# A vision-transformer block on one core: the order of the grey, edge, normalisation and projection work, and the banks of its products

## What is computed

```python
gray = einsum('bchw,c->bhw', x, (0.2989, 0.587, 0.114))
h = abs(conv(gray, scharr)).sum(over the two filters) / 2      # 3 x 3 taps, padded by one
n = (h - mean) / sqrt(var + 1e-5)                              # by row of 256
q, k, v = n @ Wq + bq, n @ Wk + bk, n @ Wv + bv                # 16 heads of 16
q, k = q @ Wp, k @ Wp                                          # in each head
h = h + softmax(q @ k.T / 4) @ v
h = h + ffn(layernorm(h))                                      # fc1, silu, fc2, dequantised weights
```

## Time and profile before

| | us |
|---|---|
| median of 3 runs | 315.38 (314.59 to 318.14) |
| profiled execution | 317.39 |
| its span in the profile | 315.6 |
| PE busy in the span | 284.4 (90%) |
| DVE busy | 206.3 (65%) |
| ACT busy | 173.8 (55%) |
| POOL busy | 136.9 (43%) |

### The profile page before, as it was taken

How to read it: one execution, slowest core, us unless ns; L and a number is a source line. 1 busy time by engine, 2 the same in 40 slices (tenths; PEclk the granted TensorE clock), 3 DMA queues, 4 the chain that set the end, 5 groups by cost and what they waited for, 6 DMA issues and landing times.

```text
span 315.6 us, 6328 instructions
## 1 busy us (share of the span) xinstructions
PE 284.4 (90%) x2332; PEld 221.0 (70%) x2332; DVE 206.3 (65%) x415; ACT 173.8 (55%) x330; POOL 136.9 (43%) x268
## 2 busy tenths in 40 slices
PE   5599059889699998899999999999999999999996
PEld 5477047767577765666666666566899899899976
DVE  8586454855699988488889888662872742641432
ACT  2416476857063378377878768768444344344450
POOL 7250534531100014766286864217859489600000
PEclk9989759999999999599999999999999999999999
DMA  6828613178979794367568000000000200200201
GB/s 213 264 61 286 185 37 137 66 223 179 322 194 316 237 335 148 92 178 225 189 160 206 11 3 2 2 0 3 0 2 0 68 2 0 70 0 0 69 0 66
DMA packets 27310, 35.90 MB, mean 114 GB/s; under 512 B 5184, under 2 KB 16272, under 8 KB 27280
## 3 DMA queue, kind: packets, MB, share of 16 engines
q1 hardware_dynamic: 27184, 35.43, 37.3%
q10 hardware_dynamic: 96, 0.07, 0.1%
HBM read 24.42 MB, written 10.49 MB: 111 GB/s over the span
## 4 chain that ended last, share of the span: by engine, by line
PE 57%; DVE 9%; DMA 8%; ACT 7%; SPq 7%; POOL 5%; issue 4%; ACTq 1%; DVEq 0%; POOLq 0%
PE bank L1198 30%; PE bank L1327 7%; PE bank L1279 6%; PE bank L1302 4%; PE bank L1307 3%; PE bank L1345 3%; DMA bv<-in_L_attn_bv 3%; DVE negmax L909 3%; DMA wscale<-in_L_ffn_fc_scales 2%; SPq L427 2%; DMA halo_x<-in_x 2%; SPq L417 2%; PE bank L1216 1%; ACT xn L1083 1%; PE bank L1337 1%
## 5 line engine op out<-in xcount | busy, mean ns | idle before, releaser
L909 DVE TENSOR_REDUCE negmax<-bank 128x2 f32<-128x512 f32 x128 | 82.1, 684 | 6.9 <-PE bank L1279 6.6
L1109 ACT ACTIVATE probs<-bank 128x512 f32<-128x512 f32 x128 | 66.3, 603 | 29.1 <-PE bank L1307 29.1
L963 DVE TENSOR_TENSOR y_l<-yf,y_h 128x512 fp32r<-128x512 f32 x32 | 24.1, 754 | 38.6 <-ACT yf L1135 38.4
L1132 ACT ACTIVATE y_h<-bank,b1col 128x512 fp32r<-128x512 f32 x32 | 22.0, 687 | 47.7 <-PE bank L1198 47.6
L1198 PE MATMUL bank<-w_h,y_h 128*128 128x256 f32 x128 | 36.9, 289 | 1.1 <-DVE y_l L963 0.7
L1198 PE MATMUL bank<-w_l,y_h 128*128 128x256 f32 x128 | 36.2, 283 | 0.0
L1198 PE MATMUL bank<-w_h,y_l 128*128 128x256 f32 x128 | 36.2, 283 | 0.0
L1327 PE MATMUL bank<-probs,vals 128*32 128x256 f32 x512 | 35.1, 393 | 0.0
L1279 PE MATMUL bank<-ks,qs 48*128 48x256 f32 x256 | 32.6, 333 | 1.3 <-DVE negmax L909 0.7
L1279 PEld LDWEIGHTS bank<-ks,qs 48*128 48x128 f32 x256 | 19.8, 189 | 15.1 <-DVE negmax L909 6.1
L1307 PEld LDWEIGHTS bank<-qs,ks 48*128 48x128 f32 x256 | 24.9, 189 | 2.7
(11 more groups left out here) (158 smaller groups left out, 609.7 us busy)
## 6 DMA issues: line engine op xcount, KB each, us to landing
xr<-in_x SPq DMA_DIRECT2D x8, 768.0 KB, 8.5
qs<-qk_parts SPq DMA_DIRECT2D x48, 128.0 KB, 3.2
ks<-qk_parts SPq DMA_DIRECT2D x48, 128.0 KB, 3.3
qk_parts<-qk_h SPq DMA_DIRECT2D x16, 256.0 KB, 3.1
qk_parts<-qk_l SPq DMA_DIRECT2D x16, 256.0 KB, 3.2
wraw<-in_L_ffn_fc_q SPq DMA_DIRECT2D x4, 512.0 KB, 5.0
wscale<-in_L_ffn_fc_scales SPq DMA_DIRECT2D x4, 512.0 KB, 6.8
out<-osb SPq DMA_DIRECT2D x16, 128.0 KB, 1.8
```

Of the source, the lines that this page charges most:

```text
L909: eng.tensor_reduce(negmax[:, b % 2, u, v], entry_bank(key)[:, :].rearrange("p (t k) -> p t k", t=NT), AX.X, ALU.max, negate=True).then_in ...
L963: eng.tensor_tensor(y_l[:, p % 2, f], yf[:, n % 2], y_h[:, p % 2, f].bitcast(fp32), ALU.subtract).then_inc(s_y, 1)
L1109: eng.activation(probs[:, n % PBUF], p2[n % 4][:, :], ACT.Exp).then_inc(s_exp, 1)
L1132: eng.activation(y_h[:, p % 2, f], src, ACT.Silu, bias=b1col[:, f:f + 1])
```

## The change

In words, by engine:

- Banks: before `qkv(0, 0)` nothing changes for the eight tiles `tok(0)` and `tok(1)` (banks 4 to 7), but the cycle over all eight banks now begins at `xt(0, 0)` instead of at `qkv(0, 0)` and runs 0 to 7 in order, not 0, 1, 2, 3, 6, 7, 4, 5. From `qkv(1, 5)` on, banks 4 to 7 are taken in the order in which they were last used. PE waits for `s_wready` before `xt(0)` and not behind it. The second `keep_busy` has 12 transposes, not 8.
- SP: images 4 and 5 are requested ahead of the halo rows of group 1; the wait for POOL's zeroed halo goes in front of `stack_halo(1)`.
- POOL: V's weights are split behind `tok_rstd(0, .)`; `tok_rstd(2, t)` goes behind the grey of image 6 + t.
- DVE: halo_add(0) behind grey 1, halo_add(1) and halo_low(1) behind the weights and `xt_low(0)`; `pick` at the end of the front part; `gray_add(6)` behind `qkv_out(0, 1)`; the second tile's statistics of pair p + 2 behind `qkv_out(p, 4)`.
- ACT: image 1's scale ahead of the halo's; the edges of tile 0 of pair 1 in two halves, one between the two normalisations; gray_scale(6) ahead of `edge(2, 0)`; `xt_high` ahead of the edge of the second tile.

```diff
@@ -266,13 +266,18 @@
                     turns.extend(("xt", p + 1, kf) for kf in range(KE))
         turn = {key: n for n, key in enumerate(turns)}
 
-        fold_over, heads_begin = turn["qkv", 0, 0], turn["qkv", 1, 5]
+        fold_over, heads_begin = turn["xt", 0, 0], turn["qkv", 1, 5]
         turn_at, nth, uses = {}, {}, [[] for r in range(8)]
         for n, key in enumerate(turns):
-            if fold_over <= n < heads_begin:
-                r = (0, 1, 2, 3, 6, 7, 4, 5)[(n - fold_over) % 8]
+            if n < fold_over:
+                r = 4 + n % 4
+            elif n < heads_begin:
+                r = (0, 1, 2, 3, 4, 5, 6, 7)[(n - fold_over) % 8]
             else:
-                r = 4 + (n if n < fold_over else n - heads_begin) % 4
+
+                if n == heads_begin:
+                    upper = sorted(range(4, 8), key=lambda q: turn[uses[q][-1]])
+                r = upper[(n - heads_begin) % 4]
             turn_at[key], nth[key] = r, len(uses[r])
             uses[r].append(key)
         last_turns = [uses[4 + q][-1] for q in range(4)]
@@ -451,11 +456,10 @@
                 eng.dma_start(qk_bcol[:, i, :], src.rearrange("(m p) -> p m", p=P), allow_slow_non_contiguous=True).then_inc(s_wpd, 16)
             eng.wait_ge(s_border, 6)
             stack_halo(eng, 0)
-            eng.wait_ge(s_halo_z, 2)
+            load_x(4)
+            load_x(5)
             load_halo(eng, 1)
-            load_x(4)
             eng.dma_start(wv_src[:], Wv.rearrange("(k p) n -> p k n", p=P)).then_inc(s_wld, 16)
-            load_x(5)
             for t in range(NT):
                 eng.dma_start(bv2[:, t, :], bv.rearrange("(a n) -> a n", a=1).broadcast_to([P, E])).then_inc(s_wld, 16)
             for b in range(6, B):
@@ -463,6 +467,7 @@
             for dst, src in ((gamma, ln_gamma), (beta, ln_beta), (b1col, fc1_bias)):
                 eng.dma_start(dst[:], src.rearrange("(m p) -> p m", p=P), allow_slow_non_contiguous=True).then_inc(s_small, 16)
             eng.dma_start(b2[:], fc2_bias.rearrange("(a n) -> a n", a=1).broadcast_to([P, E])).then_inc(s_small, 16)
+            eng.wait_ge(s_halo_z, 2)
             stack_halo(eng, 1)
 
             for i in range(4):
@@ -697,20 +702,20 @@
             for b in range(2, 4):
                 gray_high(b)
                 gray_low(b)
+            for t in range(NT):
+                tok_rstd(0, t)
             eng.wait_ge(s_wld, 16 * (NT + 1))
             link(eng.tensor_scalar(wqk_h[:, :, 2 * E:], wv_src[:], 1.0, 0.0, ALU.mult, ALU.add))
             eng.tensor_tensor(wqk_l[:, :, 2 * E:], wv_src[:], wqk_h[:, :, 2 * E:].bitcast(fp32), ALU.subtract).then_inc(s_wvready, 1)
-            for t in range(NT):
-                tok_rstd(0, t)
             for b in range(4, 6):
                 gray_high(b)
                 gray_low(b)
             for t in range(NT):
                 tok_rstd(1, t)
             for t in range(NT):
-                tok_rstd(2, t)
                 gray_high(6 + t)
                 gray_low(6 + t)
+                tok_rstd(2, t)
             for t in range(NT):
                 tok_rstd(3, t)
             split_max(0, 0)
@@ -828,22 +833,17 @@
                 eng.tensor_tensor(halo_hl[64:88, g], halo_g[:, g], halo_hl[0:24, g].bitcast(fp32), ALU.subtract).then_inc(s_halo_l, 1)
 
             gray_add(0)
-            halo_add(0)
             gray_low(0)
             gray_add(1)
+            halo_add(0)
+            gray_low(1)
             halo_low(0)
-            gray_low(1)
             halo_bands()
             gray_add(2)
             gray_add(3)
             for op in range(2):
                 eng.wait_ge(s_wt, op + 1)
                 eng.tensor_copy(wtr[:, op], bank[op][:, :]).then_inc(s_wtc, 1)
-
-            eng.wait_ge(s_ident, 1)
-            link(eng.tensor_reduce(picked[:], ident[:].rearrange("p (v c r u) -> p u v c r", v=2, c=8, r=2)[:, :, :, 0], AX.XY, ALU.add))
-            eng.tensor_copy(pick[:], picked[:]).then_inc(s_pick, 1)
-
             def weights(op):
                 scale = Q_SCALE if op == 0 else 1.0
                 eng.wait_ge(s_fold, op + 1)
@@ -976,14 +976,14 @@
                 tok_moments(p, t)
 
             tok_stats(0, 0)
-            halo_add(1)
             tok_stats(0, 1)
             for op in range(2):
                 weights(op)
-            halo_low(1)
+            halo_add(1)
             gray_add(4)
             for kf in range(KE):
                 xt_low(0, kf)
+            halo_low(1)
             gray_add(5)
             tok_stats(1, 0)
             for p in range(PAIRS):
@@ -993,15 +993,22 @@
                         largest(HEAD_AT["qkv", p, i])
                     if (p, i) == (0, 0):
                         tok_stats(1, 1)
-                    if i in TOK_AT and p + 2 < PAIRS:
-                        if p == 0 and i == TOK_AT[1]:
-                            gray_add(6)
-                        tok_stats(p + 2, TOK_AT.index(i))
-                    if i == XT_AT and p + 1 < PAIRS:
+                    if (p, i) == (0, 1):
+                        gray_add(6)
+                    if i == 1 and p + 2 < PAIRS:
+                        tok_stats(p + 2, 0)
+                    if i == 3 and p + 1 < PAIRS:
                         for kf in range(KE):
                             xt_low(p + 1, kf)
                         if p == 0:
                             gray_add(7)
+                    if i == 4 and p + 2 < PAIRS:
+                        tok_stats(p + 2, 1)
+
+            eng.wait_ge(s_ident, 1)
+            link(eng.tensor_reduce(picked[:], ident[:].rearrange("p (v c r u) -> p u v c r", v=2, c=8, r=2)[:, :, :, 0], AX.XY, ALU.add))
+            eng.tensor_copy(pick[:], picked[:]).then_inc(s_pick, 1)
+
 
 
             for s in range(END):
@@ -1064,9 +1071,9 @@
                 eng.activation(halo_hl[32:56, g], halo_g[:, g], ACT.Copy)
                 eng.activation(halo_hl[0:24, g], halo_g[:, g], ACT.Copy).then_inc(s_halo_h, 1)
 
-            def edge(p, t):
-
-                for half in range(2):
+            def edge(p, t, halves=range(2)):
+
+                for half in halves:
                     key = ("tok", p, 2 * t + half)
                     rows = slice(HALF * half, HALF * (half + 1))
                     wait_filled(eng, key)
@@ -1138,23 +1145,24 @@
             load_halo(eng, 0)
             gray_scale(0)
             gray_high(0)
+            gray_scale(1)
             halo_scale(0)
-            gray_scale(1)
+            gray_high(1)
             halo_high(0)
-            gray_high(1)
             gray_scale(2)
             gray_scale(3)
             for t in range(NT):
                 edge(0, t)
+            tok_normalise(0, 0)
+            halo_scale(1)
+            edge(1, 0, (0,))
+            tok_normalise(0, 1)
             gray_scale(4)
-            halo_scale(1)
-            tok_normalise(0, 0)
-            halo_high(1)
-            edge(1, 0)
-            tok_normalise(0, 1)
             for kf in range(KE):
                 xt_high(0, kf)
+            halo_high(1)
             gray_scale(5)
+            edge(1, 0, (1,))
             edge(1, 1)
             eng.wait_ge(s_wready, 4)
             for p in range(PAIRS):
@@ -1165,15 +1173,17 @@
                     if i == 1 and p + 1 < PAIRS:
                         for t in range(NT):
                             tok_normalise(p + 1, t)
-                    if i in TOK_AT and p + 2 < PAIRS:
-                        edge(p + 2, TOK_AT.index(i))
-                        if p == 0 and i == TOK_AT[0]:
+                        if p == 0:
                             gray_scale(6)
-                    if i == XT_AT and p + 1 < PAIRS:
+                    if i == 1 and p + 2 < PAIRS:
+                        edge(p + 2, 0)
+                    if i == 3 and p + 1 < PAIRS:
                         for kf in range(KE):
                             xt_high(p + 1, kf)
                         if p == 0:
                             gray_scale(7)
+                    if i == 3 and p + 2 < PAIRS:
+                        edge(p + 2, 1)
             neg_rows(0, 1)
 
             for s in range(SLOTS):
@@ -1392,7 +1402,7 @@
             eng.wait_ge(s_ident, 1)
             keep_busy(44, bank[0])
             eng.wait_ge(s_gray, 2)
-            keep_busy(8, bank[0])
+            keep_busy(12, bank[0])
             eng.wait_ge(s_band, 1)
             eng.wait_ge(s_border, 6)
             for t in range(NT):
@@ -1427,9 +1437,10 @@
 
             for t in range(NT):
                 tok(1, t)
+
+            eng.wait_ge(s_wready, 4)
             for kf in range(KE):
                 xt(0, kf)
-            eng.wait_ge(s_wready, 4)
             for p in range(PAIRS):
                 for i in range(6):
                     qkv(p, i)
```

## The result

The changed kernel takes 301.89 us (median of 4, 301.79 to 302.53), the kernel before beside it 315.2 (314.59 to 318.14): a ratio of 0.956, 95% interval 0.950 to 0.963. The profiled execution took 302.53, its span 300.8, 14.8 less than the 315.6 of before. Forecast were 302.4 for the median and 304.4 for the profiled execution.

What follows compares the result with a forecast made beforehand. Late inputs to PE ahead of 81.3 us, chiefly POOL's wait for V's bias, were taken as the bound. 14.1 less 1.2 for pick, called 13.0, gave 304.4 us profiled and 302.4 median; range 297.5 to 308.

Steps and rivals of the forecast that it cites:

- the likeliest case: Whole kernel: 11 to 15 us gained, 300.4 to 304.4 us; chance 0.62, including DVE blocked by POOL at 0.12.
- Start: Image 1 ahead of the halo rows: first row-tiled product 2.5 us earlier, at 13.8; edge(0,1) ends 3.0 earlier.
- First deviations and xt: Image 0's normalisation to first projection: transposes at 29.3, 12.3 us earlier; first projection at 33.1, 11.9 earlier.
- V's split at no cost: POOL splits V's weights from 28.0 to 30.0, before grey 4 at 31.6; no cost if the bias lands by 29.6.
- case (a): Rival, front part: hand-offs without slack partly give the shift back; 4 to 10 us gained, 305.4 to 311.4; chance 0.20.
- DVE held by POOL: V's split beside halo_add(1) and grey 4: POOL's 1.24 us operation delays xt_low; gain 11.8, 303.6 us; chance 0.12.
- Pairs 1 and 2: Second and third image pairs: tok(2,0) at 37.0, tok(3,0) at 53.1, 14.0 us earlier; then qkv(1,5) at 66.2.
- SP counts, not PE: Behind 81.3 the smaller shift counts: SP's head-layout reads 14.1 us earlier, against PE's 15.1 at qkv(1,5).
- pick: Moved behind DVE's last V read, its two operations make scores_by_key(0) and PE's queue wait: 1.2 us lost.
- The late wait left as it is: PE's 1.93 us wait behind the FFN weights, and half clock after it, stay, since SP and PE shift alike.
- case (b): Rival, late part: FFN weights 1.2 us earlier relative to PE, clock stays up; 1.2 + 3 more, 298.2; chance 0.12.
- Case (c): Rival, front part: PE waits of 2 to 3 us bring lasting half clock, some 25 us longer, 327; chance 0.03.

Runs made afterwards that it cites:

- The repetition: The changed kernel run once more with no edit, beside the kernel before: 301.53 us (300.23 to 301.82), ratio 0.957.

## Why the prediction was right, and where it was not

- *The median*, 302.4 forecast, 301.9 measured; the likeliest case. But the sum is right in part by luck: in the profile, two errors cancel.
- *Start.* Forecast 13.8 for the first row-tiled product, measured 13.28. Taken back, the step costs 3.5 to 3.8 us at the end, where I had 2.5 to 3: right, somewhat small.
- *First deviations and xt.* Transposes forecast 29.3, measured 29.94; the order of waits (weights at 29.7, xn 0.5 us later) is the forecast one. V's split alone, 6.1 us, and taken back, 7: this is about half of the gain.
- *V's split at no cost.* Wrong. In the profile the bias landed at 30.39 and not by 29.6, the split took 2.84 us and not 1.9, beside DVE's sums of grey 4, and POOL came to grey 4's rounding 1.1 us late; that put its residue beside DVE's grey 5, which took 0.8 more, and tok(2,0) started at 38.93 and not 37.0. I had named both causes, the late bias (in case (a)) and DVE held by POOL, with 1.24 us, and had put the second at 0.12. The repetition tells them apart: there the bias was early enough (29.19) and the split took 1.96 us, and tok(2,0) still started at 38.89, because DVE's first sum of grey 4 took 1.66 us beside it. So the cost is that of the neighbour and not of the landing. With the split behind `tok_rstd(1, .)` tok(2,0) is at 37.7.
- *Pairs 1 and 2.* With 1.9 us lost there, tok(3,0) came at 55.38 (53.1), qkv(1,5) at 68.21 (66.2), SP's reads at 51.53 (49.3). The working from tok(2,0) on was right within 0.5 us: the loss is the one above. The wait on edge(3,1) that I put in place of V's read is there, 1.74 for "about 2".
- *SP counts, not PE.* Forecast that the smaller shift counts; SP's was 11.9, PE's at qkv(1,5) 13.1, and PE was ready for the scores by key 12.4 earlier (11.8 with pick's wait). So it lies between the two, 0.5 from SP's; the chain that ended last goes through SP's queue for 16% of the span and not 7%. No experiment takes the two apart.
- *pick.* Forecast 1.2, measured 0.58. Its cast takes 0.17 and not 0.57. In the kernel before it ran beside POOL's grey residue; here POOL is idle. V's last read ends 0.24 us behind the place where PE would have begun, not 0.40.
- *The late wait left as it is.* Wrong in the profile: I said SP and PE shift alike. PE's shift at the third split is 10.4 us before its wait, the weights' 12.1, so the wait shrank by 1.7 and the half clock behind it is gone. This is case (b), given 0.12, and is worth the 3 us between 11.8 and 14.8. Of what PE lost against the weights, 0.6 us come from pick's wait, the reason given there; 1.3 come from the half clock at 98 us, which no case had. On the profiled execution the forecast 304.4 was too slow by 1.9: 1.1 lost in front, 3.0 gained there. How much of it lies in the medians isn't shown; the clock of most executions of the kernel before (above) speaks for it being there.
- *Banks.* I credited the cycle with a wait that goes and another that comes. Alone it is worth nothing (ratio 1.001), and in the changed kernel the wait for edge(3,1), taken away, comes back one product on. That step had no price of its own in the sum, and rightly.
- Case (c), a clock that stays low in the front part, did not come: 0.87 from 32 to 45 us and 1.00 from there to 94. It came for some 3 us in the repetition, behind the wait in front of qkv(1,5), and its first scores by key are at 96.98 and not 96.33.
- *The shares.* Taken back one at a time, V's place costs 6.6 to 6.9 us, image 1's order 3.5 to 3.8 and SP's order 1.0 to 1.4, together 11.1 to 12.1 of 13.3. Such shares need not add up. The other moves on ACT, DVE and POOL (the halo sums of group 1 behind the weights, the edges in halves, `tok_rstd(2, .)` behind the grey, `xt_high` ahead of the edge) were not tried alone, so what each is worth isn't shown.

## What to carry to other kernels

In a queue that runs in order, look for an operation that waits for a DMA and whose result is needed late, with an operation behind it that others wait for: moving one loop was worth about half of this whole change. A moved operation must also be checked against what the neighbouring engine does at its new place, and against the next fixed landing: an early pick gained 1.5 us at 95 us, and behind 115 us nothing was left of it. When a wait for a bank is removed, ask which bank the next product wants.

## What was not expected of the hardware

- A wait of 1.67 us on PE was followed by a stretch at half clock (0.51), and ones of 2.47 and 2.75 us too; the 3.06 us wait in front of 81.28 in the kernel before was not. The same wait in front of qkv(1,5) in the same kernel left the clock at 1.00 in one profile (1.74 us) and was followed by 0.50 in the other (1.73 us). So from the length of a wait alone these runs don't tell whether the clock falls.
- A DVE sum of two tiles (128x512) took 1.47 and 1.66 us and not 0.69 beside a POOL operation, and a cast of four columns 0.57 and not 0.17. Such delays were passed on: without V's split beside it, tok(2,0) was 1.2 us earlier and the first scores by key 1.9.
